# A transformer block on one core: where GpSimd computes the row deviations in three kinds of attention step

## The reference

```python
x = x + layernorm(attention(layernorm(x)))
x = x + layernorm(ffn(layernorm(x)))
# layernorm(x) = (x - mean) / sqrt(var + 1e-5)
# attention: kqv = x @ Wqkv + bqkv, 16 heads of 32;
#   scores = k q^T / sqrt(32), upper triangle kept, the rest -10000;
#   softmax over the key axis, times v, times Wo, plus bo
# ffn: silu(x Wg^T) * (x Wu^T), times Wd^T, weights dequantised from integers, inner size 2048
```

## Time and profile before

| | us |
|---|---|
| median of 3 runs | 1597.48 |
| lowest and highest | 1596.71, 1597.60 |
| the profiled execution, its own time | 1598.73 |
| its span | 1597.0 |
| PE busy | 1490.0 (93%) |
| DVE busy | 1120.8 (70%) |
| ACT busy | 872.7 (55%) |
| POOL busy | 798.2 (50%) |
| mean granted TensorE clock, share of full | 0.982 |

### The profile page before, as it was taken

How to read it: one execution, slowest core, us unless ns; L and a number is a source line. 1 busy time by engine, 2 the same in 40 slices (tenths; PEclk the granted TensorE clock), 3 DMA queues, 4 the chain that set the end, 5 groups by cost and what they waited for, 6 DMA issues and landing times.

```text
span 1597.0 us, 24894 instructions
## 1 busy us (share of the span) xinstructions
PE 1490.0 (93%) x9032; PEld 613.6 (38%) x9032; DVE 1120.8 (70%) x2151; ACT 872.7 (55%) x1444; POOL 798.2 (50%) x982
## 2 busy tenths in 40 slices
PE   4899999989999899899999899999999999999997
PEld 2333334333333333333333233444444444444443
DVE  5757855688766787756777657777677677767765
ACT  5345765666566567566667655552465155604441
POOL 4325754676675676666576535552355235421112
PEclk8999999999999999999999999999999999999999
DMA  5321242123332223321335642226121612161002
GB/s 185 93 54 33 62 93 54 28 76 100 85 95 77 84 66 94 98 55 26 100 98 160 188 98 83 82 87 171 50 89 47 159 50 100 37 145 40 14 1 79
DMA packets 149628, 133.26 MB, mean 83 GB/s; under 512 B 95617, under 2 KB 99713, under 8 KB 149249
## 3 DMA queue, kind: packets, MB, share of 16 engines
q1 hardware_dynamic: 149504, 131.67, 29.4%
HBM read 53.76 MB, written 31.46 MB: 53 GB/s over the span
## 4 chain that ended last, share of the span: by engine, by line
PE 71%; POOL 12%; DVE 7%; issue 5%; ACT 4%; DMA 0%; POOLq 0%; DVEq 0%; ACTq 0%
PE ps L1202 23%; PE ps L1098 16%; PE ps L1161 11%; PE ps L1243 7%; PE ps L1219 5%; PE ps L1135 5%; POOL pt L1823 4%; DVE mcol L1560 3%; PE ps L1111 2%; POOL rs L1723 1%; POOL pt L1814 1%; POOL stage L1807 1%; PE ps L1119 1%; ACT pt L1359 1%; PE ps L1228 1%
## 5 line engine op out<-in xcount | busy, mean ns | idle before, releaser
L1359 ACT ACTIVATE pt<-ps,nrm 128x512 f32<-128x512 f32 (+1 forms) x640 | 361.1, 645 | 227.0 <-PE ps L1135 200.5
L1560 DVE TENSOR_REDUCE mcol<-ps 128x1 f32<-128x512 f32 (+2 forms) x600 | 305.7, 576 | 148.6 <-PE ps L1119 74.8
L1823 POOL TENSOR_TENSOR pt<-pt 128x1024 f32<-128x1024 f32 x84 | 200.3, 2408 | 1.8 <-ACT pt L1359 1.8
L1161 PE MATMUL ps<-pt,v 128*32 128x512 f32 (+3 forms) x1536 | 188.4, 501 | 0.9 <-DVE rec L1592 0.9
L1814 POOL TENSOR_SCALAR_AFFINE_SELECT pt<-pt 128x256 f32<-128x256 f32 (+1 forms) x192 | 96.4, 509 | 167.6 <-ACT pt L1359 166.5
L1135 PE MATMUL ps<-qpack,kpack 98*128 98x512 f16 (+3 forms) x768 | 162.7, 334 | 14.7 <-DVE mcol L1560 11.1
L1161 PE MATMUL ps<-pt,ones 128*32 128x512 f32 (+3 forms) x1200 | 115.4, 476 | 33.5 <-POOL pt L1814 33.2
L1807 POOL TENSOR_TENSOR stage<-tq,stage 128x512 f16<-128x512 f32 x64 | 74.0, 1157 | 145.0 <-ACT tq L1332 144.9
L1202 PE MATMUL ps<-x2t,sw 128*128 128x512 f16 x512 | 131.5, 380 | 2.8 <-DVE yy L1678 2.8
L1202 PE MATMUL ps<-x2t,gu 128*128 128x512 f16 x512 | 131.6, 380 | 2.2 <-ACT part L1381 2.0
L1202 PE MATMUL ps<-x2even,gu 128*128 128x512 f16 x512 | 131.5, 380 | 1.7 <-DVE hf L1452 1.7
(11 more groups left out here) (163 smaller groups left out, 2592.7 us busy)
## 6 DMA issues: line engine op xcount, KB each, us to landing
qpack<-stage SPq DMA_DIRECT2D x192, 64.0 KB, 2.0
kpack<-stage SPq DMA_DIRECT2D x192, 64.0 KB, 2.0
xr<-in_x SPq DMA_DIRECT2D x32, 256.0 KB, 2.8
x1d<-xr SPq DMA_DIRECT2D x32, 256.0 KB, 2.4
x2d_t<-xh SPq DMA_DIRECT2D x32, 256.0 KB, 2.0
x1in<-x1d SPq DMA_DIRECT2D x32, 256.0 KB, 2.8
out_x<-yy SPq DMA_DIRECT2D x32, 256.0 KB, 2.1
xin<-in_x SPq DMA_DIRECT2D x24, 256.0 KB, 3.1
```

The costliest lines, as they stand in the source:

```text
L1161: mm = pe.matmul((DEN if kind == "den" else NUM)[rows, q0:512], heads, Pt[:, ks, h, at:at + 512 - q0], start=kb_ == (first_den(n, j) if ki ...
L1359: act.activation(Pt[:, PBUF[step], h, off:512], ps[:, BANK[job], off:512], ACT.Exp, scale=esc).then_inc(s_ex, 1)
L1560: mm = dve.tensor_reduce(mcol[:, n % 2, col:col + 1], scores, AX.X, ALU.max)
L1823: pool.tensor_tensor(Pt[:, 2, h:h + 2, :], Pt[:, 2, h:h + 2, :], Pt[:, PBUF[STEP[a[:3]]], h:h + 2, :], ALU.add).then_inc(s_sum, 1)
```

## The change

In steps 1, 2 and 7 the deviations that are due are put into the list behind the four scores of the step, and no longer at the step's head. In the other seven kinds of step they stay. For GpSimd this moves them behind that step's two masks, and also behind the halves (step 1) or a sum (step 7). No other engine's order changes, no instruction is added or removed, and the order of the deviations among themselves stays, so the semaphore values are the same.

```diff
+LATE_DEVS = (1, 2, 7)
...
             here = rows.get(NS * n + s, [])
             add(("step", n, s))
-            plan += [("dev", "residual", job[1]) for job in here if job[0] == "dev2"]
-            plan += [("dev", DEV_FOR[job[0]], job[1]) for job in here if job[0] in DEV_FOR]
+            devs = [("dev", "residual", job[1]) for job in here if job[0] == "dev2"]
+            devs += [("dev", DEV_FOR[job[0]], job[1]) for job in here if job[0] in DEV_FOR]
+            if s not in LATE_DEVS:
+                plan += devs
...
             plan += [("score", n, j, kb, h) for h in range(4)]
+            if s in LATE_DEVS:
+                plan += devs
```

## The result

| | before | after |
|---|---|---|
| median of 4 runs, us | 1597.12 | 1608.10 |
| lowest to highest | 1596.71 to 1597.60 | 1607.40 to 1608.85 |
| the profiled execution, its own time | 1598.73 | 1608.19 |
| its span | 1597.0 | 1606.5 |

The ratio is 1.0063 with a 95% interval of 1.0051 to 1.0075, which is 10.1 us. It is 11 us in the medians and 9.5 us in the two profiled executions. The forecast was +7.6 us, 1605.1 us in a range of 1595 to 1611.5.

What follows compares the result with a forecast made beforehand. PE, with 71% of the chain, was taken to bound the kernel, waiting for GpSimd's masks. Terms 6.8 + 2.6 + 0.4 + 1.1 + 0.5 + 0.2 − 4.0 gave +7.6 us: 1597.48 to 1605.1 us, range 1595 to 1611.5.

Steps and rivals of the forecast that it cites:

- the main term: Stages 5 and 9: late deviations delay ACT, and PE's product starts 3.4 us later in each, +6.8 us.
- the cast's chain: In 5,2 to 5,4: late normalisations delay evacuations, cast, DVE's lower half and normalisation, then PE's product: 393.95 instead of 390.53.
- The direct gains: Steps 4,1, 8,1 and 12,1: PE waits less for masks, ACT's slack hides the late normalisation; −1.2, −1.6, −1.2, together −4.0 us.
- Stages 6 and 10: The 2.2 us gained at the masks are eaten by the late evacuation of bank 5; +0.2 us each, +0.4.
- Step 7: Stages 4, 8, 12, 13, 15: PE's 1.2 us gain is lost waiting for DVE's L1566 at the transpose; 0, but +0.2 in 12,7.
- The sum: All terms over the whole kernel: +7.6 us, median from 1597.48 to 1605.1 us.
- The terms of step 1: Late step 1 deviations: 5,1 delays the exponentials of 5,2 by 0.9 us; stages 4, 8, 12 gain 4.0; stage 13 loses 0.5.
- A: Rival, faster: ACT's lateness is absorbed and direct gains stand, 13 us less, 1584.4 us; chance 0.13.
- B: Rival, no change: later waits swallow both gains and losses, 1597.5 us; chance 0.09.
- C: Rival, more loss: ACT's lateness pushes step 8 in stages 4, 8, 12, 13; stages 6, 10 lose too; +13.6, 1611.1 us; chance 0.12.
- The signs named in advance: Changed profile: PE waits less for masks, ACT more for deviations; 5,3 over 3 us later; stages 4, 8, 12 over 1 us shorter.

Runs made afterwards that it cites:

- slack1: Against the kernel before: only the deviations of step 1 in stages 4, 8 and 12 put behind the masks; ratio 0.9973, −4.3 us.
- late2: Against the kernel before: only the deviations of step 2 put behind the masks (eleven steps); ratio 1.0056, +9.0 us.
- late7: Against the kernel before: only the deviations of step 7 put behind the masks (five steps); ratio 0.9994, −1.0 us.
- late1: Against the kernel before: only the deviations of step 1 put behind the masks (seven steps); ratio 1.0013, +2.1 us.
- evacfirst: The changed kernel with normalisations of steps 1 and 2 behind the projection's evacuations; ratio 0.9994 against the kernel before, −1.0 us.

## Why the prediction was right, point by point

**The sign and the main term** were right and for the reason given. The chain of 5,2 was worked out to PE's `num` at 393.95; less the 0.97 us by which the profiled execution was ahead at that stage's start, it is 392.98, and the trace has 392.91. The last of the three deviations was due at 386.3 by the same shift and ended at 386.44. Stage 5 lost 3.1 us up to step 4 (forecast 3.4), stage 1 2.2 (2.6), stage 2 0.8 (1.1). Stage 9, which was to repeat stage 5, lost only 2.1.

**What the forecast called the cast's chain is two things,** and their weights were not told apart by it. It named the projection only as agreeing in sign. The runs show that the order on ACT is the whole loss (11 us go with the evacuations ahead, 12.6 with the lower half on GpSimd), and that taking DVE's lower half away saves 1.8 us, or 3.4 once the evacuations are ahead. In the trace the projection waits first (3.52 us) and DVE's chain adds 1.14.

**The direct gains** of stages 4, 8 and 12 were −4.0 by the forecast and −4.3 by slack1, and that match is partly luck. In 4,2 PE's products start at 321.68 instead of 322.84, 1.2 us as forecast, but from step 3 on only 0.75 us are left, and the same in stage 12. In 8,2 PE's wait falls by 1.2 us and not by 1.6. In the profiles these shortfalls are made up by 1.6 us in 8,2, where the products and scores run at the full clock in place of the lower one, and the forecast had no such term.

**Stages 6 and 10** were said to have their 2.2 us eaten at bank 5. In stage 6 they were: the projection of 6,3 starts at 452.00 behind a wait of 2.27 us for the evacuation (L1350), which is 448.9 and the 3.0 us that the stage had come late, plus 0.1. What the stage lost beyond it fell in the stretch of lower clock. Stage 10 has the same wait of 2.27 us, and then the wait for a transfer, 1.1 us, which the forecast hadn't.

**Step 7** gave nothing, as forecast: −1.0 us with zero in the interval. The reason given was half of it.

**The sum** was low: +7.6 against +10 to +11. Most of what is missing lies in step 1. late2 alone measured +9.0 where its terms give 8.2 (1.7 + 1.1 + 5.0 + 0.4), and late7 −1.0 where they give 0.2. That leaves +2.1 for step 1, as late1 measured alone, where the forecast has 7.6 − 8.2 − 0.2 = −0.8. The terms of step 1 were too small by the way over GpSimd's L1814, which I hadn't seen; but how much of that remains when step 2 is late too was not tried by itself, and each of these figures has an interval of about 1 to 2 us to either side.

**The rivals.** A (lateness absorbed, −13 us) was wrong with ACT's program as it is. With its order changed the loss goes, but A's gain doesn't come: evacfirst is level, with the lower half moved −4.3. That ACT is busy 54% of the time said nothing on it. B is excluded by the result. C (+13.6 us) isn't excluded by its size: the measured +10 to +11 lies midway between it and the forecast. Its picture isn't what the runs show: step 7 costs nothing (late7), and the waits at bank 5 in stages 6 and 10 eat the gain and no more.

**The signs named in advance:** PE's wait for masks fell to 13.7 us, "well under half" of 33.2; ACT's waits grew to 25.0; `num` of 5,4 waits for `rec`; L797 in 5,3 starts at 389.17 against 386.70, 3.4 us later when the 0.97 us are added. In stage 1 `num` waits 1.14 us for `rec` too, in stage 9 it doesn't. Two signs came out the other way. The products behind 8,1 don't start right behind L1118 but 1.37 us later. And the stages 4 and 12 got shorter by 1.0 and 0.9 us where over 1 us was asked for; for that case the forecast had said that the gain terms are wrong and the time lies above 1608 us, and it lies at 1608.1.

## What to carry to other kernels

In a queue that runs in order, an instruction that waits holds up everything behind it. Before a producer is moved back, list what stands behind its first consumer on the consumer's engine, and who waits for that: here a normalisation with a user a step away stood ahead of the evacuation that frees PE's only projection bank. Move only those producers whose consumers are far, or put the urgent work ahead of the consumer first; the same move then went from 10 us lost to level and, with the second user freed as well, to 4 us won; a chosen part of it won about 10, of which some 6 remain at an equal clock. A busy share of 54% says nothing on whether an engine may be late.

## What the runs showed of the hardware

The join of 128x16 values with two inputs in SBUF took 1017 ns on average and up to 1666 beside GpSimd's sums and lower halves, and 175 ns beside none; as a reduction with one input of 128x64 it took 217 ns on average, and 211 to 223 in all 16 places. Short stretches at the lower clock of TensorE come back at much the same places in kernels that differ by the order of a few instructions (near 121 and 411 us in nearly all profiles), but single ones come and go: those at 196 and 551 us stand only before, those at 451, 530 and 871 us only after. Stage 7, of some 54 us, looked 1.7 us longer for such a stretch alone. The expectations had taken no account of it.
